# A decoder layer: routed tokens made on ScalarE and turned by the DMA, experts chosen on VectorE, layer norms applied on ScalarE

## The chip, the cores and the metric

One core of one Trainium2 chip. The metric is the device time of one execution in microseconds, the median of several runs. Another execution was profiled; its rows are quoted below.

## What is computed

A decoder layer on 2048 tokens (32 x 64) of width 256, in float32. Three parts, each on a layer norm of x and each added to x:

```python
x = x + attn(layernorm(x))          # 16 heads of 16; rope; each token's heads attend to each other (bshd,bstd->bsht)
x = x + xattn(layernorm(x), ctx)    # 16 heads, 2048 keys; q, k, v and the probabilities quantised to 8 bits
x = x + moe(layernorm(x))           # 8 experts of hidden 128, the best 2 of a token, and a shared one

scores = sigmoid(xt @ gate.T); sel = top_k(scores + expert_bias, 2)
xb = bfloat16(xt * score)           # the token times the score of each chosen expert
h = silu(xb @ w1[e].T) * (xb @ w3[e].T); out_r = h @ w2[e].T
hs = silu(xt @ shared_w1.T) * (xt @ shared_w3.T); out = hs @ shared_w2.T + sum of out_r
```

## The kernel before

**Tiles and lags.** The tokens are 16 tiles of 128. The keys and values are made first (some 100 us); then `over_tiles` runs `body(t)` for t = 0 to 17 on every engine. In `body(t)` the cross attention of tile t runs through its 16 heads h, and around it lies the work of other tiles: a = t + 2 (norm 0, own attention), n = t + 1 (own attention's end, norm 1, the queries), m = t - 1 (end of the cross attention, norm 2, the gates), o = t - 2 (the experts, the output). Each engine has its list, written by hand: for every h, in which order the calls for t, a, n, m and o stand. An engine goes through its list in order; semaphores tie the lists together. Norms are numbered 0, 1, 2 (`kind`).

**A head.** TensorE makes scores(h, 0) and scores(h, 1), each 128 tokens by 1024 keys, in one of two PSUM slots. VectorE evicts both to `score` with the running minimum (L1178) and makes the exponent's bias (L1188). ScalarE's `exp_head` (L865) makes 16-bit probabilities; `score` and `prob` are rings of 4. SP's `turn` (L431) issues a DMA transpose of 128x2048 two-byte elements for each head into one of 6 buffers. `times_values` (L1558) multiplies four heads at a time by the values.

**Norms.** VectorE gathers the statistics. GpSimd's `ln_scale` makes variance + eps (L462), its power -1/2 (L466) and, for all three norms (`POOL_NORMS`), the normed tokens `normed` (L482). TensorE turns them (`ln_turn`), ScalarE copies them to `normed_t` (`ln_keep`). After `ln_turn(1, n)` at h = 12 come `xq` (L1386 and L1502), VectorE's `largest_query` and `quantise_queries` at h = 13, TensorE's `q_turn`, and ScalarE's `keep_queries`.

**Own attention on GpSimd.** `rope`, then eight products of 128x1024 elements (L594), each folded twice (L604, L612); `reduce_scores` and `largest_score` on VectorE (h = 11, 14, 15) and `shift_scores` on GpSimd stand before ScalarE's `head_exp`, after which come the four value products. `spread_sums(m)`, among them, needs VectorE's `cross_sum(m)` (L1195, h = 3).

**Experts.** `gate_and_shared` at h = 10 gives the gate's logits and the shared hidden layer; ScalarE takes a tanh of each. GpSimd's `choose` ranks the eight scores with twelve small instructions on 128x64 elements at most. TensorE's `spread_gates` (L1605, h = 13 and 14) multiplies each expert's column, spread to 128 columns, with the identity, so that the gate of every token lies along a row of all partitions; ScalarE copies it (`keep_gates`, h = 12 and 13), and GpSimd's `route` multiplies the turned tokens `normed_t` by it into `routed_t` (two products of 128x1024). The last tile does this on VectorE (`choose_last`, L1210 to L1222, and `route_last`). `experts(i, j)` (L1386, 8 bf16 matmuls each) makes the first (j = 0) and the second (j = 1) hidden product of four experts: (0,0) at h = 14, (0,1) and (1,0) at h = 0 of the next tile, (1,1) at h = 1. ScalarE's `hidden_tanh(0)` stands at h = 14, `hidden_tanh(1)` at h = 0 ahead of that head's exp; VectorE's `expert_hidden(0)` at h = 0 and `(1)` at h = 1; `experts_out` and `add_out` at h = 2.

Of the kernel before, what the change touches and what calls it, by code (L numbers as in the profile page):

```python
# [45 lines left out]
P = 128  # L46
# [17 lines left out]
POOL_NORMS = (0, 1, 2)  # L64
# [37 lines left out]
def by_dma(n):  # L102
    return n % H in BY_DMA
# [32 lines left out]
def layer_kernel(nc, a):  # L136
    with ExitStack() as ctx:
# [14 lines left out]
        earlier = sb("earlier", [P, E, E])  # L152
# [87 lines left out]
        gate = sb("gate", [P, 3, E])  # L240
        ahead = sb("ahead", [P, E, E])
        beats = sb("beats", [P, E, E])
        ties = sb("ties", [P, E, E])
        routed_gate = sb("routed_gate", [P, E])
        last_gate = sb("last_gate", [P, 4, E])

        routed_both = sb("routed_both", [P, 2, E * D], BF16)
        gate_wide = routed_both[:, 0, :].bitcast(F32).rearrange("p (e q) -> p e q", e=E)
# [110 lines left out]
        last_chain = sem("last_chain")  # L359
        gate_spread = sem("gate_spread")  # L360
        gate_kept = sem("gate_kept")
        routed_kept = sem("routed_kept")
# [19 lines left out]
        def _(sp):  # L382
# [15 lines left out]
            for buf, name in ((w_o, "w_o"), (w_xq, "w_xq"), (b_xq, "b_xq"), (w_p, "w_p"),  # L398
                              (b_p, "b_p"), (w_gate, "w_gate"), (b_expert, "b_expert"),
                              (earlier, "earlier"), (w_s1, "w_s1"), (w_s3, "w_s3"),  # L400
                              (w_s2, "w_s2")):
                sp.dma_start(buf[:], a[name]).then_inc(w_loaded, 16)
# [29 lines left out]

            def body(t):
                for h in range(H):
                    if t.exists() and by_dma(h):
                        turn(h, t)
                    if h == 9 and (t + 3).exists():
                        load_x(t + 3)
                    if h == 4 and (t + -2).exists():
                        store(t + -2)  # L440
# [8 lines left out]
        def _(pool):  # L449
# [5 lines left out]
            def ln_scale(kind, t):  # L455
# [3 lines left out]
                if kind not in POOL_NORMS and (due := t.due(1)) is not None:  # L459
# [22 lines left out]
                pool.tensor_scalar(normed[:, kind, :], x, mean_var[:, kind, 0:1], rstd[:, kind:kind + 1],  # L482
                                   ALU.subtract, ALU.mult).then_inc(ln_done[kind], 1)
# [27 lines left out]

            def choose(t):


                pool.wait_ge(gate_tanhed, t.count(1, 1))
                pool.sem_inc(settled, 1)
                if (due := t.due(2)) is not None:
                    pool.wait_ge(gate_spread, due)
                    pool.sem_inc(settled, 1)
                sig, biased, rank = gate[:, 0, :], gate[:, 1, :], gate[:, 2, :]  # L520
                mine = biased.unsqueeze(2).to_broadcast([P, E, E])
                others = biased.unsqueeze(1).to_broadcast([P, E, E])
                pool.tensor_scalar(sig, gate_tanh[:], 0.5, 0.5, ALU.mult, ALU.add).then_inc(gate_chain, 1)
                pool.wait_ge(gate_chain, t.count(12, 1))
                pool.sem_inc(settled, 1)
                pool.tensor_tensor(biased, sig, b_expert[:], ALU.add).then_inc(gate_chain, 1)
                pool.wait_ge(gate_chain, t.count(12, 2))
                pool.sem_inc(settled, 1)
                pool.tensor_tensor(ahead[:], others, mine, ALU.subtract).then_inc(gate_chain, 1)
                pool.wait_ge(gate_chain, t.count(12, 3))  # L530
                pool.sem_inc(settled, 1)
                pool.tensor_scalar(ties[:], ahead[:], 0.0, None, ALU.is_equal).then_inc(gate_chain, 1)
                pool.tensor_scalar(beats[:], ahead[:], 0.0, None, ALU.is_gt).then_inc(gate_chain, 1)
                pool.wait_ge(gate_chain, t.count(12, 5))
                pool.sem_inc(settled, 1)
                pool.tensor_tensor(ties[:], ties[:], earlier[:], ALU.mult).then_inc(gate_chain, 1)
                pool.wait_ge(gate_chain, t.count(12, 6))
                pool.sem_inc(settled, 1)
                pool.tensor_tensor(beats[:], beats[:], ties[:], ALU.add).then_inc(gate_chain, 1)
                pool.wait_ge(gate_chain, t.count(12, 7))  # L540
                pool.sem_inc(settled, 1)
                pool.tensor_tensor(ties[:, :, 0:4], beats[:, :, 0:4], beats[:, :, 4:8], ALU.add
# [1263 lines left out]
```

## Time and profile before

| what | value |
|---|---|
| median of 3 runs | 1085.49 us (1084.84 to 1087.52) |
| the profiled execution | 1091.66 us, span 1089.9 us |
| VectorE (DVE) busy | 906.8 us, 83% |
| GpSimd (POOL) busy | 854.3 us, 78% |
| TensorE (PE) busy | 754.3 us, 69% |
| ScalarE (ACT) busy | 686.6 us, 63% |
| DMA transposes | 256 |

A busy time is the sum of an engine's instructions; a wait is shown with the instruction before which the engine stood idle, and with what released it.

### The profile page before, as it was taken

How to read it: one execution, taken by the hardware profiler on the slowest of the kernel's cores; microseconds unless marked ns; L12 is line 12 of the kernel's file. 1: busy time of each engine (PE TensorE's matmuls, PEld its weight loads, DVE VectorE, ACT ScalarE, POOL GpSimd, SP SyncE). 2: the span in 40 equal slices, each digit the busy share in tenths (PEclk: the TensorE clock that was granted, in tenths of full speed). 3: DMA queues.
4: the chain of work that ended last, by engine and by line, in shares of the span. 5: the costliest groups of instructions: out<-in, count | busy, mean ns of one | idle time of the engine just before them, and what ended most of it. 6: DMA issues, size and time to landing. Idle time of an engine off the chain costs nothing.

```text
span 1089.9 us, 21862 instructions
## 1 busy us (share of the span) xinstructions
PE 754.3 (69%) x7250; PEld 438.0 (40%) x7328; DVE 906.8 (83%) x1802; ACT 686.6 (63%) x843; POOL 854.3 (78%) x874
## 2 busy tenths in 40 slices
PE   7956667676667577676656777676768677677565
PEld 4533314344334344344333444344334344334244
DVE  4996889797979889796979889696978889798983
ACT  2534667675757667575768667575666667567761
POOL 7658989797988979797989979797988979763030
PEclk9975779897979989797989879797988979788988
DMA  6012879686986969596877869596876969588991
GB/s 221 1 39 66 163 130 171 125 166 116 167 146 121 168 117 167 111 168 118 163 143 138 159 117 172 106 168 117 162 146 118 178 115 168 97 160 150 165 175 24
DMA packets 540888, 147.71 MB, mean 136 GB/s; under 512 B 534116, under 2 KB 538727, under 8 KB 540391
## 3 DMA queue, kind: packets, MB, share of 16 engines
q1 hardware_dynamic: 540774, 146.31, 72.4%
q8 instruction: 58, 0.95, 0.4%
q14 instruction: 56, 0.45, 0.1%
HBM read 9.96 MB, written 2.10 MB: 11 GB/s over the span
## 4 chain that ended last, share of the span: by engine, by line
issue 31%; POOL 29%; PE 19%; DVE 16%; ACT 2%; POOLq 1%; DMA 1%; SPq 0%; DVEq 0%; ACTq 0%
POOL product L594 14%; DVE score L1178 8%; PE ps L1605 4%; PE ps L1386 4%; POOL normed L482 3%; PE ps_score L1528 3%; POOL folded L612 3%; POOL rstd L466 2%; POOL qk_sin L581 2%; PE ps_score L1386 2%; POOL qk_rot L583 2%; PE ps L1502 1%; PE ps L1507 1%; DVE q_parts L1161 1%; PE ps L1391 1%
## 5 line engine op out<-in xcount | busy, mean ns | idle before, releaser
L1178 DVE TENSOR_SCALAR_CACHE_REDUCE score<-ps_score,q_neg 128x1024 f32<-128x1024 f32 x512 | 636.4, 1276 | 92.6 <-PE ps_score L1528 92.6
L865 ACT ACTIVATE prob<-score,exp_bias 128x2048 uint16<-128x2048 f32 x256 | 512.1, 2001 | 100.8 <-DVE exp_bias L1188 94.5
L1528 PE MATMUL ps_score<-keys,queries 128*128 128x512 bf16 x946 | 319.9, 424 | 178.7 <-DVE score L1178 165.2
L1528 PEld LDWEIGHTS ps_score<-keys,queries 128*128 128x128 bf16 x1024 | 77.7, 103 | 308.9 <-DVE score L1178 239.3
L604 POOL TENSOR_TENSOR folded<-product 128x512 f32<-128x512 f32 x128 | 158.7, 1263 | 2.7 <-DVE hs L1114 1.7
L594 POOL TENSOR_TENSOR product<-hs_exp,v_tok 128x1024 f32<-128x1024 f32 x64 | 149.7, 2353 | 1.6 <-ACT hs_exp L830 1.6
L594 POOL TENSOR_TENSOR product<-qk_rot 128x1024 f32<-128x1024 f32 x64 | 149.0, 2342 | 0.2 <-POOL qk_rot L587 0.2
L567 POOL TENSOR_TENSOR routed_both<-normed_t,routed_both 128x1024 bf16<-128x1024 f32 x30 | 70.6, 2356 | 33.7 <-ACT routed_both L916 33.2
L612 POOL TENSOR_TENSOR folded<-folded 128x256 f32<-128x256 f32 x128 | 92.6, 746 | 0.0
L1391 PE MATMUL ps<-ident,normed 128*128 128x128 f32 x96 | 24.8, 347 | 89.1 <-POOL normed L482 82.5
L809 ACT COPY normed_t<-ps 128x256 f32<-128x256 f32 x48 | 17.6, 366 | 100.8 <-PE ps L1391 100.8
L1558 PEld LDWEIGHTS ps_pv<-prob_t,values 128*32 128x32 f16 x4096 | 60.1, 99 | 31.6 <-issue 31.6
L1558 PE MATMUL ps_pv<-prob_t,values 128*32 128x128 f16 x4096 | 71.4, 224 | 1.9 <-DMA prob_t<-prob 1.9
L1188 DVE TENSOR_SCALAR exp_bias<-low 128x1 f32<-128x1 f32 x256 | 53.9, 210 | 5.3 <-issue 0.3
L1391 PEld LDWEIGHTS ps<-ident,normed 128*128 128x128 f32 x96 | 12.0, 164 | 109.6 <-POOL normed L482 100.8
L916 ACT COPY routed_both<-ps 128x512 f32<-128x512 f32 x30 | 17.4, 584 | 60.0 <-PE ps L1605 59.7
L1386 PE MATMUL ps<-routed_both,w 128*128 128x128 bf16 x512 | 41.4, 227 | 18.2 <-POOL routed_both L567 13.9
L1605 PE MATMUL ps<-ident,routed_gate 128*128 128x128 f32 x256 | 54.0, 398 | 0.0
L1605 PEld LDWEIGHTS ps<-ident,routed_gate 128*128 128x128 f32 x256 | 52.1, 310 | 0.1
L1386 PEld LDWEIGHTS ps<-routed_both,w 128*128 128x128 bf16 x512 | 33.2, 102 | 41.5 <-POOL routed_both L567 28.8
L865 ACT ACTIVATION_READ_ACCUMULATOR prob<-score,exp_bias 128x1 f32 x256 | 48.2, 188 | 0.0
L462 POOL TENSOR_SCALAR var_eps<-mean_var 128x1 f32<-128x1 f32 x48 | 12.8, 267 | 38.8 <-DVE mean_var L1106 37.8
(138 smaller groups left out, 1216.2 us busy)
## 6 DMA issues: line engine op xcount, KB each, us to landing
prob_t<-prob SPq DMA_TRANSPOSE x256, 4.5
prob_t<-in_w SPq DMA_DIRECT2D x3, 1024.0 KB, 4.8
x_in<-in_x SPq DMA_DIRECT2D x16, 128.0 KB, 3.0
score<-in_cond_t SPq DMA_DIRECT2D x4, 512.0 KB, 6.9
out<-x_out SPq DMA_DIRECT2D x16, 128.0 KB, 2.5
w_qkv<-in_w_qkv SPq DMA_DIRECT2D x1, 768.0 KB, 4.2
early<-in_w_kv SPq DMA_DIRECT2D x1, 512.0 KB
w_s<-in_w_s SPq DMA_DIRECT2D x3, 128.0 KB
```

What stands on the lines that cost most here:

```text
L567: pool.tensor_tensor(routed_t[:, EG * i:EG * i + EG], normed_t[:, 2].unsqueeze(1).to_broadcast([P, EG, C, P]), gate_wide[:, EG * i:EG * i ...
L594: pool.tensor_tensor(product[:, i % 2], a_, b_, ALU.mult).then_inc(multiplied, 1)
L604: pool.tensor_tensor(folded[:, r], product[:, r, :, :, 0:HD // 2], product[:, r, :, :, HD // 2:HD], ALU.add).then_inc(fold_done, 1)
L612: pool.tensor_tensor(folded[:, r, :, :, 0:HD // 4], folded[:, r, :, :, 0:HD // 4], folded[:, r, :, :, HD // 4:HD // 2], ALU.add).then_inc( ...
L865: act.activation(prob[:, s, :].bitcast(U16), score[:, s, :], ACT.Exp, bias=exp_bias[:, s:s + 1], scale=-1.0, accum_out=prob_sum[:, t.par, ...
L1178: dve.tensor_scalar(score[:, s, HALF * i:HALF * i + HALF], ps_score[:, score_slot(t.count(H, h), i)].rearrange("p b k -> p (b k)"), q_neg[ ...
L1188: dve.tensor_scalar(exp_bias[:, s:s + 1], low[:, s, 0:1], low[:, s, 1:2], LN255, ALU.min, ALU.add).then_inc(bias_ready, 1)
L1386: mm = pe.matmul(out, lhs[c], rhs[c], start=start and c == 0, stop=stop and c == C - 1)
L1391: mm = pe.transpose(out[:, P * c:P * c + P], src[:, P * c:P * c + P], ident[:])
L1528: mm = pe.matmul(ps_score[:, score_slot(n, i), b, :], queries[:, t.par, h // 2, h % 2, :], keys[:, h // 2, k0:k0 + KEYS], start=True, stop ...
L1558: mm = pe.matmul(out[j], beside_zeros(values, i, h + j), prob_t[:, t.count(H, h + j) % KEPT, i, :], start=(i == 0 and first), stop=(i == T ...
L1605: mm = pe.matmul(bank[6 + i][:, P * e:P * e + P], routed_gate[:, EG * i + e:EG * i + e + 1] .to_broadcast([P, P]), ident[:], start=True, s ...
```

## The change

Four parts:

- `choose` runs on VectorE for every tile, at h = 10 ahead of the bias, with the six steps that `choose_last` had (the largest two by `max` and `match_replace`). GpSimd's `choose` and its table `earlier` go.
- `route(e, m)` is eight instructions on ScalarE, four at h = 12 and four at h = 13, each ahead of that head's exp: expert e's copy of the tokens `normed` (not turned), scaled by row. SP's `turn_routed(m)`, at h = 13 ahead of `turn(13)`, turns all eight by one DMA transpose of 128x2048 bf16. `spread_gates`, `keep_gates`, GpSimd's `route` and `route_last` go.
- GpSimd's `ln_scale` ends with a 128x1 `shift`; ScalarE's `ln_apply` makes `normed`: norm 0 at h = 1, norm 2 at h = 8, norm 1 at h = 10.
- The experts' calls stand later: `experts(0,0)` and `(0,1)` at h = 0 ahead of scores(0,0), `(1,0)` at h = 0, `(1,1)` at h = 2; `hidden_tanh(0)` and `(1)` at h = 1 and 2, ahead of those heads' exp; `expert_hidden(0)` and `(1)` at h = 1 (ahead of the evictions) and h = 2 (behind them); `experts_out` and `add_out` at h = 3; the store at h = 5. `queries_or_keys(0)` moves from h = 3 to h = 4, and `sum_turn` waits for `ln_keep(0)` of tile t + 3.

The core of the diff:

```diff
@@
+            def turn_routed(t):
+
+                sp.wait_ge(routed_made, t.count(E, E))
+                sp.sem_inc(settled, 1)
+                if (due := t.due(4)) is not None:
+                    sp.wait_ge(hidden_made, due)
+                    sp.sem_inc(settled, 1)
+                sp.dma_start_transpose(routed_t.rearrange("p e c q -> p (e c) q"),
+                                       routed_tok.rearrange("p e d -> p (e d)")).then_inc(routed_turned, 16)
+
             def body(t):
                 for h in range(H):
+                    if (t + -1).exists() and h == 13:
+                        turn_routed(t + -1)
...
-                if kind not in POOL_NORMS:
-                    pool.tensor_scalar(shift[:, kind:kind + 1], mean_var[:, kind, 0:1],
-                                       rstd[:, kind:kind + 1], -1.0, ALU.mult, ALU.mult
-                        ).then_inc(ln_shifted[kind], 1)
-                    return
-                if kind > 0:
-                    pool.wait_ge((one_done, two_done)[kind - 1], t.count(1, 1))
-                    pool.sem_inc(settled, 1)
-                if (due := t.due(1)) is not None:
-                    pool.wait_ge(ln_turned[kind], due)
-                    pool.sem_inc(settled, 1)
-                x = (x_in[:, t.par, :], x_one[:, t.par, :], x_two[:])[kind]
-                pool.tensor_scalar(normed[:, kind, :], x, mean_var[:, kind, 0:1], rstd[:, kind:kind + 1],
-                                   ALU.subtract, ALU.mult).then_inc(ln_done[kind], 1)
+                pool.tensor_scalar(shift[:, kind:kind + 1], mean_var[:, kind, 0:1],
+                                   rstd[:, kind:kind + 1], -1.0, ALU.mult, ALU.mult
+                    ).then_inc(ln_shifted[kind], 1)
...
+            def route(e, t):
+
+                if e == 0:
+                    act.wait_ge(gate_chain, t.count(6, 6))
+                    if (due := t.due(16)) is not None:
+                        act.wait_ge(routed_turned, due)
+                act.activation(routed_tok[:, e, :], normed[:, 2, :], ACT.Copy, scale=routed_gate[:, e:e + 1]
+                               ).then_inc(routed_made, 1)
...
-                    if o.exists() and h == 0:
-                        hidden_tanh(1, o)
+                    if o.exists() and h in (1, 2):
+                        hidden_tanh(h - 1, o)
...
+                    if m.exists() and h in (12, 13):
+                        for e in range(EG * (h - 12), EG * (h - 12) + EG):
+                            route(e, m)
...
+                    if m.exists() and h == 8:
+                        ln_apply(2, m)
+                    if n.exists() and h == 10 + late:
+                        ln_apply(1, n)
...
+                    if a.exists() and h == 1 + behind:
+                        ln_apply(0, a)
...
-                    if o.exists() and h == 0:
+                    if o.exists() and h == 1:
                         expert_hidden(0, o)
...
+            def experts(i, j, t):
+
+                b = ((5, 6), (7, 5))[i][j]
+                pe.wait_ge(routed_turned, t.count(16, 16))
+                if i == 1 and j == 0:
+
                     pe.wait_ge(shared_chain, t.count(2, 2))
-                for e in range(EG):
-                    mm = pe.matmul(bank[6 + i][:, P * e:P * e + P], routed_gate[:, EG * i + e:EG * i + e + 1]
-                                   .to_broadcast([P, P]), ident[:], start=True, stop=True)
-                mm.then_inc(gate_spread, 1)
-
-            def experts(i, j, t):
-
-                b = ((5, 6), (7, 5))[i][j]
-                pe.wait_ge(routed_kept, t.count(2, i + 1))
+                if i == 0 and j == 1:
+
+                    pe.wait_ge(two_done, t.count(1, 1))
...
                     if o.exists() and h == 0:
+                        experts(0, 0, o)
                         experts(0, 1, o)
                     if t.exists():
                         scores(h, 0, t)
...
-                    if m.exists() and h == 14:
-                        experts(0, 0, m)
```

VectorE's new `choose(t)` is the old `choose_last(t)` of the listing above with `gate` for `last_gate`, a count of 6 a tile on `gate_chain`, and for its last step a wait for the routes of the tile before.

## Rows read from the trace of the kernel before

**Rows 1.** Windows of one tile; busy time (instructions) by engine, granted clock, DMA share
```profile
core 0: us, PE busy (x) PEld busy (x) DVE busy (x) ACT busy (x) POOL busy (x), PEclk, DMA share, GB/s
249.78:311.25 61.47, 41.96 (x455) 24.75 (x449) 52.48 (x107) 41.20 (x51) 53.37 (x56) 0.89 0.81 142
...
864.06:925.48 61.42, 45.30 (x505) 26.90 (x511) 52.85 (x110) 41.51 (x52) 53.41 (x56) 0.88 0.79 146
```

**Rows 2.** The chain of waits, tile 6: start us, us, what
```profile
503.52 0.85 PE ps_score L1528 x2
504.38 1.71 PE ps L1386 x4
...
509.71 1.03 PE ps L1507 x8
510.75 3.31 PE ps L1605 x16
```

**Rows 3.** The timeline of VectorE, tiles 6 and 7, with idle time before
```profile
495.64 0.69 DVE L1114 TENSOR_REDUCE hs<-folded 128x128 f32<-128x512 f32 x1 [0.71 <-POOL folded L612]
...
504.42 1.28 DVE L1178 TENSOR_SCALAR_CACHE_REDUCE score<-ps_score,q_neg 128x1024 f32<-128x1024 f32 x1 [3.83 <-PE ps_score L1528]
...
507.27 0.43 DVE L1142 TENSOR_REDUCE ps<-ps 128x16 f32<-128x256 f32 x1 [1.31 <-PE ps L1502]
...
514.53 1.28 DVE L1178 TENSOR_SCALAR_CACHE_REDUCE score<-ps_score,q_neg 128x1024 f32<-128x1024 f32 x1 [2.22 <-PE ps_score L1528]
...
522.03 1.28 DVE L1178 TENSOR_SCALAR_CACHE_REDUCE score<-ps_score,q_neg 128x1024 f32<-128x1024 f32 x1
...
531.85 0.24 DVE L1195 RECIPROCAL sum_inv<-prob_sum 128x16 f32<-128x16 f32 x1
...
550.98 1.28 DVE L1178 TENSOR_SCALAR_CACHE_REDUCE score<-ps_score,q_neg 128x1024 f32<-128x1024 f32 x1
...
553.64 1.27 DVE L1178 TENSOR_SCALAR_CACHE_REDUCE score<-ps_score,q_neg 128x1024 f32<-128x1024 f32 x1
```

**Rows 4.** The timeline of GpSimd, tiles 6 and 7
```profile
502.86 0.20 POOL L523 TENSOR_SCALAR gate<-gate_tanh 128x8 f32<-128x8 f32 x1
...
507.88 2.47 POOL L604 TENSOR_TENSOR folded<-product 128x512 f32<-128x512 f32 x2
...
518.84 2.36 POOL L567 TENSOR_TENSOR routed_both<-normed_t,routed_both 128x1024 bf16<-128x1024 f32 x1
...
529.68 0.22 POOL L462 TENSOR_SCALAR var_eps<-mean_var 128x1 f32<-128x1 f32 x1
...
530.97 1.24 POOL L482 TENSOR_SCALAR normed<-x_in,mean_var,rstd 128x256 f32<-128x256 f32 x1 [0.31 <-POOL rstd L466]
...
534.48 0.52 POOL L509 COPY sum_wide<-sum_inv 128x128 f32<-128x128 f32 x2
```

**Rows 5.** The timeline at the end, the choice of the last tile and its experts
```profile
1076.88 0.17 DVE L1210 TENSOR_SCALAR last_gate<-gate_tanh 128x8 f32<-128x8 f32 x1 [5.30 <-ACT gate_tanh L904]
...
1077.89 0.17 DVE L1222 SCALAR_TENSOR_TENSOR routed_gate<-last_gate 128x8 f32<-128x8 f32 x1
...
1081.57 1.75 PE L1386 MATMUL ps<-routed_both,w 128*128 128x128 bf16 x24 [0.33 <-DVE routed_both L1229]
```

**Rows 6.** The timeline of ScalarE, tile 6
```profile
513.08 2.04 ACT L847 COPY queries<-ps 64x1024 bf16<-64x1024 bf16 x2
...
518.91 0.42 ACT L830 ACTIVATE hs_exp<-hs 128x256 f32<-128x256 f32 x1 [0.71 <-POOL hs L488]
519.24 1.99 ACT L865 ACTIVATE prob<-score,exp_bias 128x2048 uint16<-128x2048 f32 x1
```

**Rows 7.** The DMA queues (packets, MB, share) and `prob_t`'s transposes
```profile
q1 hardware_dynamic: 540774, 146.31, 72.4%
...
DMA to landing us min/median/max: 4.2/4.5/7.5
```

**Rows 8.** The timeline near the end: expert matmuls, the tanh behind them
```profile
1056.34 1.06 PE L1386 MATMUL ps<-routed_both,w 128*128 128x128 bf16 x16
...
1060.12 0.58 ACT L923 ACTIVATE early<-ps 128x512 f32<-128x512 f32 x1
```

More of the change, by code:

```diff
@@ L63 @@
 TURN = 2
-POOL_NORMS = (0, 1, 2)
 BY_DMA = tuple(range(H))
@@ L458, in ln_scale @@
                 pool.sem_inc(settled, 1)
-                if kind not in POOL_NORMS and (due := t.due(1)) is not None:
+                if (due := t.due(1)) is not None:
                     pool.wait_ge(ln_done[kind], due)
@@ L668, in body @@
                     ln_scale(1, n)
-                if m.exists() and t.exists():
-                    choose(m)
                 if a.exists():
@@ L975, in _ @@
             first, second = Tile(0), Tile(1)
-            if 0 not in POOL_NORMS:
-                ln_apply(0, first)
+            ln_apply(0, first)
             ln_keep(0, first)
@@ L984, in _ @@
                     head_exp(first)
-                if u == 5 and 0 not in POOL_NORMS:
+                if u == 5:
                     ln_apply(0, second)
@@ L994, in _ @@
                 if u == 9:
-                    if 1 not in POOL_NORMS:
-                        ln_apply(1, first)
+                    ln_apply(1, first)
                     ln_keep(1, first)
@@ L1204, in cross_norm, with choose @@
                                   xo_raw[:].rearrange("p c q -> p (c q)"), ALU.mult).then_inc(xo_done, 1)
-            def choose_last(t):
-                sig, biased, marked, best = (last_gate[:, i, :] for i in range(4))
+            def choose(t):
+                sig, biased, marked, best = (gate[:, i, :] for i in range(4))
                 dve.wait_ge(gate_tanhed, t.count(1, 1))
-                dve.tensor_scalar(sig, gate_tanh[:], 0.5, 0.5, ALU.mult, ALU.add).then_inc(last_chain, 1)
-                dve.wait_ge(last_chain, 1)
+                dve.tensor_scalar(sig, gate_tanh[:], 0.5, 0.5, ALU.mult, ALU.add).then_inc(gate_chain, 1)
+                dve.wait_ge(gate_chain, t.count(6, 1))
@@ L1325, in body @@
                         ln_combine(1, n)
-                    if o.exists() and h == 1:
+                    if o.exists() and h == 2:
                         expert_hidden(1, o)
-                    if m.exists() and not t.exists() and h == 14:
-                        route_last(1, m)
-                    if m.exists() and not t.exists():
-                        if h == 10:
-                            choose_last(m)
-                        if h == 13:
-                            route_last(0, m)
-                    if o.exists() and h == 2:
+                    if m.exists() and h == 10:
+                        choose(m)
+                    if o.exists() and h == 3:
                         add_out(o)
@@ L1646, in body @@
                         pe.wait_ge(values_half, 2)
-                    if m.exists() and h == 14:
-                        spread_gates(1, m)
                     if o.exists() and h == 0:
+                        experts(0, 0, o)
                         experts(0, 1, o)
@@ L1688, in body @@
                         times_values(3 * G, m)
-                    if m.exists() and h == 13:
-                        spread_gates(0, m)
                     if a.exists() and h == 4 + behind:
+                        queries_or_keys(0, a)
                         queries_or_keys(1, a)
-                    if a.exists() and h == 3 + behind:
-                        queries_or_keys(0, a)
                     if t.exists() and h == 7:
```

143 lines of the change are left out of this document (25 added, 118 removed).

## The prediction

> **What bounds the kernel now.** I start with the windows, one for each tile of the main loop [rows 1]. Eleven neighbouring ones last about 61.45 us each; VectorE is busy for 52.5 of them, GpSimd for 53.4, TensorE for 42, ScalarE for 41, and the DMA engines for 0.8 of the time. The two busiest each have some 8 us idle in every tile, so the pace is set by a ring of waits and not by one full engine. The chain of waits of one tile [rows 2] gives the ring: GpSimd's layer norm 1 (its end is 502.8, where `choose` begins [rows 4]), TensorE's turn of it, the scores and `xq`, VectorE's `quantise_queries`, `q_turn`, `spread_gates`, then VectorE up to `largest_score` and back to GpSimd. VectorE's timeline has what it waited in this tile [rows 3]: 0.71, 3.83, 1.31 and 2.22 us, all on that ring. 61.45 - 8.07 = 53.4 us is what VectorE needs for a tile without waits. A plain head (two evictions and a bias) is 553.64 - 550.98 = 2.66 of it.
>
> **What leaves, per tile.** GpSimd [rows 4]: the twelve instructions of `choose`, 502.86 to 507.88, 5.0 us; two `route` products of 2.36; and each of three norms ends with a 128x1 instruction in place of a 128x256 one: 1.24 + 0.31 of hand-over against 0.22 (as `var_eps`) + 0.2, so 1.1 less. Its own work falls from 53.4 to about 40. TensorE: the 16 f32 matmuls of `spread_gates`, 3.31 on the ring [rows 2].
>
> **What comes.** VectorE: `choose`, which the last tile already runs as `choose_last`, 1076.88 to 1078.06 = 1.18 us [rows 5]. ScalarE: three `ln_apply` and eight `route`, 128x256 f32 each, priced by `hs_exp` of that shape: 0.42 long, the next instruction starts 0.33 after it [rows 6]. That is 3.6 us a tile, less two gate copies; from 41 it doesn't fill ScalarE. DMA: a 17th transpose of 128x2048 two-byte elements. One takes 4.2 to 7.5 us to land, median 4.5 by the issues' list, and occupies 0.724 x 1089.9 / 256 = 3.1 us of the 16 DMA engines [rows 7]; 17 are 52 us a tile, not full either. On SP the new one stands ahead of `turn(13)`, whose probabilities are made after the routed tokens, so nothing waits behind it.
>
> The Trainium skill (DMA: Bandwidth & Descriptors, section Latency and other measured facts) gives DMA transposes 261 GB/s in a non-contiguous case, an estimate of 2.0 us for these 0.52 MB. The trace doesn't agree (3.1 us). By the page the wait B below would be 1.1 shorter and the result 13 us lower.
>
> **The new ring.** Engines are in order, so I follow the calls' new places through one steady tile, in four pieces.
>
> A, from `shift` of norm 1 on GpSimd to VectorE being ready for head 0 of the next tile. ScalarE has `ln_apply(1)` at h = 10 ahead of `gate_tanhs`, and VectorE has `choose` at h = 10 ahead of bias(10): so VectorE now waits there for GpSimd's norm 1. Apply 0.35, tanh 0.25, choose 1.18, bias 0.13: at 1.9. Head 11 with `reduce_scores` 0.6 and `shared_hidden` 0.53: 5.7. Head 12: 8.3. TensorE stood idle until 3.8 and then runs at the slow clock, as after the long wait of before [rows 2]: scores 0.85, turn 0.7 (502.8 to 503.5), scores 0.85 and `keep` 0.4, `xq` 2.9 (504.38 to 507.27): the product is there at about 9.1, so VectorE waits 0.8. Quantise 2.4 (507.27 to 509.71), heads 13, 14, 15 at 2.66, one reduce 0.6, `largest_score` 0.34: 20.3.
>
> B, the new wait at h = 0. `experts(0,0)` and `(0,1)` stand ahead of scores(0,0) on TensorE and need the whole transpose. `q_turn` is done at 12.5, ScalarE's `keep_queries` takes 2.04 [rows 6], four routes 1.4: 16.0. SP issues, 4.5 to land: 20.6. Sixteen expert matmuls 1.06 [rows 8], the first scores 0.6: 22.4. VectorE wanted them at 20.3: 2.1 late; 1.8 with the fastest landing of the trace, 5.1 with the slowest.
>
> C, from there to `cross_sum` at h = 3. Before: 522.03 to 531.85 = 9.8 [rows 3]. `expert_hidden(0)` has moved behind head 0: +1.3. It needs `hidden_tanh(0)`, which stands on ScalarE behind exp_head(0), and that one waits for bias(0) of VectorE: so VectorE stands for an exp 2.0 [rows 6], a tanh 0.6 [rows 8] and the hand-overs, 2.7 us. `expert_hidden(1)` needs a tanh behind exp_head(1) and `keep_xo` (2.1 + 0.3 + 0.6 + 0.1), against 2.4 of evictions: 0.7 more. C is 14.5.
>
> D, GpSimd from there to `shift` of norm 1. Before: 534.48 [rows 4] to 502.8 + 61.45 = 564.25, 29.8 with two norms and no wait inside; less 2 x 1.1: 27.6. `choose` and the routes stood behind norm 1, so D doesn't get shorter by them. The stretch from `largest_score` to `spread_sums` does, but there GpSimd now waits for `cross_sum`, which hangs on C: what it saves turns into idle time.
>
> Sum: 20.3 + 2.1 + 14.5 + 27.6 = 64.5, against 61.45: +3.05 a tile. From the other side: VectorE's 53.4 + 1.2, and waits of 2.1 (B), 2.7 and 0.7 (C), 0.8 (xq), and 3.7 at `choose`, where VectorE is at 14.5 + 7 x 2.66 + 3.5 of other work + 2.4 = 39.0 after head 0 and the tanh at 42.1 + 0.6: 64.6. Twelve tiles (2 to 13) have all of it: +37.
>
> The ends. Tiles 0 and 1: fewer norms on GpSimd, -2, and the first B, +2. Tile 14: 2.7 + 0.7 + 1.3 + 2.1, less a wait behind `spread_gates` as the 2.22 of [rows 3]: +4.6. Tile 15: 4.7, less some 1.3 of waits for `route`: +3.4. After the last head, `hidden_tanh(1)`, `expert_hidden(1)` and `experts_out` of tile 14 lie in front of `cross_norm` (0.6 + 1.4 + 0.6 and hand-overs, +3); the last norm is 0.7 shorter; and from `choose` to the experts there are eight routes and a transpose, 2.7 + 4.6, where there were 1081.57 - 1078.06 = 3.5 [rows 5]: +3.8. Together +6.
>
> 37 + 0 + 4.6 + 3.4 + 6 = +51. The profiled execution took 1091.66 (span 1089.9 and 1.8 around it), its like would take 1143; it lies 6 above the median of the runs, 1085.49, and on that the forecast is 1136.
>
> **Rivals.**
> 1. The transpose is hidden: B is 0, the ring 62.4, +11 for twelve tiles and +13 at the ends, 1110. For it: the DMA queue is free at that point. Against: the routes stand behind `keep_queries`, which ends at 14.6 of A's 20.3, and a landing takes 4.2 at least.
> 2. VectorE becomes the bound and the new waits on it are small: faster. It waited 8.07; with 1.2 for `choose`, the kernel is faster as soon as the new waits sum to under 6.9 a tile. With 2 us of them a tile is 56.6, 58 us less over twelve, 1040 with the ends. For it: GpSimd loses 13 of its 53.4 us. Against: the 2.7 at h = 1 follows from the order of calls alone, and with B and 0.7 there are 5.5 before GpSimd comes in.
> The Trainium skill (Perfetto Trace Analysis, section Identifying the Most-Contended Engine) takes the engine with the highest occupancy for the one to relieve; here it is GpSimd by 1 us, and the page by itself would point to this rival.
> 3. GpSimd has slack that I don't see: VectorE's own chain with C and B, 62.2, +9 and +15 at the ends, 1110.
> 4. Transposes crowd each other and land near 7.5, and TensorE, idle more often, is granted the slow clock in more places: the ring is 67.5, 1172.
>
> **Numbers.** Forecast 0.60, rivals 1 and 3 together 0.17, rival 2 0.11, rival 4 0.12. Rivals 1 and 3 are slower by 2%; errors in both at once give no change, which I take 0.05 for. A measurement of this kernel tells 0.3% (3.3 us) from none. So faster 0.12, within 0.3% 0.05, slower 0.83. The range for 8 in 10 leaves out rival 2 and the far end of 4: 1100 to 1165.
>
> **What would show it.** In the changed trace: tiles of 64 to 65 us; GpSimd busy about 40 of each, with its longest wait before `sum_wide`; VectorE idle 2.7 us at h = 1 before `early`, released by ScalarE's tanh; VectorE idle before head 0, released by scores that stood behind the experts; VectorE idle some 3.7 before `gate`, released by `gate_tanh`; and no wait of 3.8 us before head 12. I am wrong if a tile is under 61.4 us, above all if the tanh at h = 1 is there when VectorE asks for it, or the transpose has landed when TensorE gets to the experts.

## The result, and the profile after

| what | before | after |
|---|---|---|
| median | 1086.03 us (1084.84 to 1087.52, 4 runs) | 1180.36 us (1178.57 to 1187.96, 4 runs) |
| ratio | | 1.0881, interval 1.083 to 1.0933 |
| profiled execution | 1091.66 us, span 1089.9 | 1178.77 us, span 1177.0 |
| VectorE, GpSimd busy | 906.8, 854.3 us | 917.2, 693.0 us |
| granted TensorE clock, mean | 0.865 | 0.806 |

Slower, as forecast, but by 94 us and not by 51; the time is above the range. Some runs of a kernel fall into a slower state of the chip: the medians below count them and the ratios don't, which bears on `norms_alone` alone, where two of six did. The changed kernel's windows of one tile, with the columns of [rows 1]:

```profile
core 0: us, PE busy (x) PEld busy (x) DVE busy (x) ACT busy (x) POOL busy (x), PEclk, DMA share, GB/s
474.54:540.63 66.09, 43.59 (x372) 23.58 (x360) 51.72 (x110) 43.31 (x60) 42.54 (x41) 0.84 0.78 139
540.63:608.12 67.49, 44.92 (x433) 23.82 (x436) 53.63 (x117) 44.73 (x60) 42.81 (x41) 0.80 0.78 137
```

A tile takes 66.1 and 67.5 us where it took 61.45. GpSimd did lose load: 42.5 of a tile instead of 53.4. (The forecast had 40: it took 5.0 off for `choose`, which is its time with the gaps between the instructions; `choose_alone` below shows 3.0 of work.) VectorE, now the busiest engine of a tile, stands idle for 14 us of each instead of 9. Its timeline shows where, with the idle time and its releaser in the brackets. The lines with a wait over 0.25 us are shown, and two more; those between are left out. It answers to [rows 3]:

```profile
525.64 0.17 DVE L1137 TENSOR_SCALAR gate<-gate_tanh 128x8 f32<-128x8 f32 x1 [4.03 <-ACT gate_tanh L828]
533.41 0.43 DVE L1069 TENSOR_REDUCE ps<-ps 128x16 f32<-128x256 f32 x1 [0.17 <-PE ps L1417]
547.59 1.28 DVE L1105 TENSOR_SCALAR_CACHE_REDUCE score<-ps_score,q_neg 128x1024 f32<-128x1024 f32 x1 [2.69 <-PE ps_score L1443]
553.32 0.69 DVE L1155 SCALAR_TENSOR_TENSOR early<-early,ps 128x512 f32<-128x512 f32 x1 [2.78 <-ACT early L849]
561.62 0.69 DVE L1155 SCALAR_TENSOR_TENSOR early<-early,ps 128x512 f32<-128x512 f32 x1 [1.76 <-ACT early L849]
563.08 0.24 DVE L1122 RECIPROCAL sum_inv<-prob_sum 128x16 f32<-128x16 f32 x1
592.31 0.17 DVE L1137 TENSOR_SCALAR gate<-gate_tanh 128x8 f32<-128x8 f32 x1 [4.36 <-ACT gate_tanh L828]
```

These are the waits that the prediction named: at `choose` 4.03 (forecast 3.7), before head 0 2.69 (2.1), the first tanh 2.78 (2.7), the second 1.76 (0.7; the mean of ten tiles is 1.96). The waits of 3.83, 2.22 and 0.71 of [rows 3] are gone, and the one before `quantise_queries` is 0.17 instead of 1.31. The wait before head 0 can be followed back through TensorE's and ScalarE's timelines and the list of issues:

```profile
538.77 1.71 ACT L842 ACTIVATE routed_both<-normed,routed_gate 128x256 bf16<-128x256 f32 x4
...
545.53 1.16 PE L1301 MATMUL ps<-routed_both,w 128*128 128x128 bf16 x16 [2.22 <-DMA routed_both<-routed_both]
```

```profile
540.63 4.85 DMA routed_both<-routed_both
545.53 1.16 PE ps L1301 x16
546.70 0.87 PE ps_score L1443 x2
...
552.69 0.60 ACT early L849
553.32 0.70 DVE early L1155
```

```profile
DMA to landing us min/median/max: 4.3/4.7/5.6
```

The second fence is the chain of waits, and the third the transposes of the routed tokens, against 4.2/4.5/7.5 of [rows 7]. The last routes end at 540.48; the transpose is on its way from 540.63 and takes 4.85, with TensorE waiting for it; the experts run, and only then the scores that VectorE wants.

On GpSimd the time saved is a wait, as the prediction's D has it. Three lines of its timeline, answering to [rows 4]:

```profile
524.64 0.26 POOL L474 TENSOR_SCALAR shift<-mean_var,rstd 128x1 f32<-128x1 f32 x1 [0.20 <-POOL rstd L470]
542.09 0.62 POOL L481 TENSOR_TENSOR hs<-hs,hs_max 128x256 f32<-128x256 f32 x1 [10.51 <-DVE hs_max L1046]
563.58 0.52 POOL L502 COPY sum_wide<-sum_inv 128x128 f32<-128x128 f32 x2 [4.72 <-DVE sum_inv L1122]
```

It waits for `largest_score` (10.5) and for `cross_sum` (4.7): about 15 us that the lighter GpSimd gives back in one tile.

The four pieces of the ring, as means of ten tiles (3 to 12), cut at instructions of VectorE's and GpSimd's timelines. Piece A is counted here from the start of norm 1's `rstd`, some 1 us before the end of its `shift`, so in these terms the forecast A is 21.3 and D 26.6.

| piece, us | before | forecast | after |
|---|---|---|---|
| A, norm 1 to VectorE ready for head 0 | 20.06 | 21.3 | 20.98 |
| B, to the start of head 0's eviction | 1.41 | 2.1 | 2.82 |
| C, to `cross_sum` | 9.89 | 14.5 | 15.68 |
| D, GpSimd to the next norm 1 | 30.06 | 26.6 | 27.18 |
| a tile | 61.42 | 64.5 | 66.66 |

(Before, B held `expert_hidden(0)`, which belongs to C after.) The spans differ by 87.1: tiles 2 to 13 +64.0 (forecast 37), tile 14 +7.0 (4.6), tile 15 +9.6 (3.4), what follows it +9.8 (6), tiles 0 and 1 +1.0 (0), the part before the loop -4.3. The prediction had nothing for that last one.

### The profile page after: what moved, and what is told of

Its sections match the earlier page's. It is cut to its first block, busy times and chain, and to the rows that moved or that the text cites. A ratio compares the mean times of both kernels' runs of the same rounds, so it can differ in the third digit from the quotient of the medians.

```text
span 1177.0 us, 21273 instructions
## 1 busy us (share of the span) xinstructions
PE 782.0 (66%) x7072; PEld 424.2 (36%) x7072; DVE 917.2 (78%) x1905; ACT 750.1 (64%) x989; POOL 693.0 (59%) x664
## 4 chain that ended last, share of the span: by engine, by line
issue 24%; DVE 23%; PE 19%; POOL 18%; ACT 8%; DMA 7%; SPq 1%; POOLq 0%; DVEq 0%; ACTq 0%
DVE score L1105 13%; POOL product L527 10%; DMA routed_both<-routed_both 6%; PE ps L1301 6%; PE ps_score L1443 4%; PE ps_pv L1473 2%; ACT routed_both L842 2%; POOL qk_sin L514 2%; POOL folded L545 2%; DVE early L1155 2%; PE ps_score L1301 2%; ACT queries L771 2%; ACT early L849 2%; POOL qk_rot L516 1%; POOL rstd L470 1%
## 5 line engine op out<-in xcount | busy, mean ns | idle before, releaser
L1443 PE MATMUL ps_score<-keys,queries 128*128 128x512 bf16 x1024 | 378.8, 466 | 256.9 <-DVE score L1105 249.6
L481 POOL TENSOR_TENSOR hs<-hs,hs_max 128x256 f32<-128x256 f32 x16 | 9.9, 621 | 149.4 <-DVE hs_max L1046 149.4
L1473 PE MATMUL ps_pv<-prob_t,values 128*32 128x128 f16 x4096 | 92.2, 261 | 3.2 <-DMA prob_t<-prob 3.2
L1473 PEld LDWEIGHTS ps_pv<-prob_t,values 128*32 128x32 f16 x4096 | 78.8, 118 | 34.5 <-issue 34.5
L502 POOL COPY sum_wide<-sum_inv 128x128 f32<-128x128 f32 x32 | 8.4, 291 | 139.7 <-DVE sum_inv L1122 139.7
L1155 DVE SCALAR_TENSOR_TENSOR early<-early,ps 128x512 f32<-128x512 f32 x32 | 22.0, 687 | 84.2 <-ACT early L849 74.0
L1301 PE MATMUL ps<-routed_both,w 128*128 128x128 bf16 x512 | 53.6, 278 | 46.9 <-DMA routed_both<-routed_both 45.3
L1301 PEld LDWEIGHTS ps<-routed_both,w 128*128 128x128 bf16 x512 | 46.6, 129 | 72.5 <-DMA routed_both<-routed_both 56.2
L842 ACT ACTIVATE routed_both<-normed,routed_gate 128x256 bf16<-128x256 f32 x128 | 54.2, 494 | 0.3
L1137 DVE TENSOR_SCALAR gate<-gate_tanh 128x8 f32<-128x8 f32 x16 | 2.7, 172 | 58.4 <-ACT gate_tanh L828 58.4
```

The source lines that it names most:

```text
L842: act.activation(routed_tok[:, e, :], normed[:, 2, :], ACT.Copy, scale=routed_gate[:, e:e + 1]).then_inc(routed_made, 1)
L1155: dve.scalar_tensor_tensor(out=th, in0=th, scalar=1.0, in1=first_, op0=ALU.add, op1=ALU.mult).then_inc(chain, 1)
L1301: mm = pe.matmul(out, lhs[c], rhs[c], start=start and c == 0, stop=stop and c == C - 1)
L1443: mm = pe.matmul(ps_score[:, score_slot(n, i), b, :], queries[:, t.par, h // 2, h % 2, :], keys[:, h // 2, k0:k0 + KEYS], start=True, stop ...
L1473: mm = pe.matmul(out[j], beside_zeros(values, i, h + j), prob_t[:, t.count(H, h + j) % KEPT, i, :], start=(i == 0 and first), stop=(i == T ...
```

## The experiments

**Theory 1:** the order of calls makes the ring. Three calls stand ahead of something that VectorE needs sooner: `ln_apply(1)`, which waits for GpSimd, ahead of the gate's tanh; the experts, which wait for the DMA, ahead of the scores; `expert_hidden(0)`, which waits for ScalarE, ahead of the evictions. **Theory 2:** the parts cost time by themselves: VectorE's extra work, the extra transpose, ScalarE's extra instructions. **Theory 3:** TensorE's lower granted clock is what went beyond the forecast. All ratios are to the kernel before on the same chip (its own median moves by a few us between chips), with 95% intervals; the changed kernel's is 1.0881.

**One move each, and all three.** They undo nothing of the four parts and only change the place of a call.

```diff
+ gate_first: ScalarE, h = 10, behind gate_tanhs and shared_tanhs instead of ahead
+                    if n.exists() and h == 10 + late:
+                        ln_apply(1, n)
+ scores_first: TensorE, h = 0, behind scores(0, 0) and scores(0, 1) instead of ahead
+                        experts(0, 0, o)
+                        experts(0, 1, o)
                         experts(1, 0, o)
+ evict_first: VectorE, h = 1, behind the evictions instead of ahead
+                    if o.exists() and h == 1:
+                        expert_hidden(0, o)
```

> The changed kernel, with one call moved on ScalarE: norm 1's apply stands behind the two gate tanhs at h = 10 and no longer ahead of them. Theory 1 (the order of calls on the ring): VectorE stands before `choose` for 4.0 to 4.4 us in every tile for GpSimd's norm 1 only because of that place. Without it `choose`, head 11 and half of head 12 run while GpSimd works; the queries then come about 2.9 us sooner in the ring, 12 to 13 times: 1180 falls by some 36, to 1144 (range 1130 to 1155). Theory 2 (the engines themselves: ScalarE's and the DMA's added work, or the slow TensorE clock, cost the time, wherever the calls stand): the wait moves to the queries and nothing is gained, 1175 to 1185.

> The changed kernel, with the experts' first two products on TensorE at h = 0 behind that head's scores and no longer ahead of them. Theory 1: the wait for the DMA of the routed tokens (2.2 us idle, 2.8 with the matmuls) no longer holds VectorE's head 0; the experts are still done before ScalarE gets to their tanh. 2.8 a tile, in 14 tiles: minus 39, to 1141 (1130 to 1155). Theory 2: the transpose lands late because of DMA traffic and everything behind the experts waits just as long: 1175 to 1185, with the idle time of VectorE now before `early`.

> The changed kernel, with VectorE's first expert product at h = 1 behind that head's two evictions and no longer ahead of them. Theory 1: the 2.78 us idle before it (bias(0), exp, tanh) is covered by 2.4 us of evictions; `cross_sum` and with it GpSimd come 2.4 us sooner in 14 tiles: minus 33, to 1147 (1135 to 1160). Theory 2: the wait moves to the second expert product or to TensorE, 1175 to 1185.

> All three moves at once: gate tanhs ahead of norm 1's apply, scores ahead of the experts, evictions ahead of the first expert product. Theory 1: the gains add as long as the ring stays the bound, 2.9 + 2.8 + 2.4 = 8.1 a tile, until VectorE's own work (53.4 + 1.2) and its small waits bound it at some 58: 1075 to 1090, level with the kernel before or a little faster. Theory 2 (the engines): above 1150.

| kernel | median us | ratio | A | B | C | D |
|---|---|---|---|---|---|---|
| `gate_first` | 1153.19 | 1.0616 [1.0568, 1.0663] | 18.41 | 3.08 | 15.80 | 27.19 |
| `scores_first` | 1145.68 | 1.0544 [1.0514, 1.0574] | 21.31 | 0.10 | 15.57 | 27.19 |
| `evict_first` | 1135.38 | 1.0463 [1.0387, 1.0539] | 21.03 | 2.54 | 12.61 | 27.19 |
| `all_three` | 1077.07 | 0.9927 [0.99, 0.9954] | 18.59 | 0.10 | 13.52 | 27.22 |

Each move shortens the piece that it was aimed at, by 2.6, 2.7 and 3.1 us, and leaves the others within 0.4. The gains are 27, 35 and 45 us, 107 in sum; together they give 103, and the kernel with the whole change is then 0.7% faster than the one before. VectorE's waits, in total, times and longest, of `gate_first`, `scores_first`, `evict_first` and `all_three`, after those of the changed kernel:

```profile
DVE early L1155 <- ACT early L849: 74.0, 30, 7.3
DVE gate L1137 <- ACT gate_tanh L828: 58.4, 15, 4.8
DVE score L1105 <- PE ps_score L1443: 58.1, 47, 4.1
```

```profile
DVE early L1155 <- ACT early L849: 75.4, 29, 7.0
DVE score L1105 <- PE ps_score L1443: 60.6, 41, 4.9
...
DVE gate L1137 <- ACT gate_tanh L828: 4.8, 1, 4.8
```

```profile
DVE early L1155 <- ACT early L849: 71.9, 29, 6.9
DVE gate L1137 <- ACT gate_tanh L828: 58.5, 15, 4.8
DVE score L1105 <- PE ps_score L1443: 21.8, 37, 3.1
```

```profile
DVE score L1105 <- PE ps_score L1443: 59.2, 46, 4.2
DVE gate L1137 <- ACT gate_tanh L828: 58.5, 15, 4.8
DVE early L1155 <- ACT early L849: 28.2, 17, 7.0
```

```profile
DVE early L1155 <- ACT early L849: 37.5, 16, 7.0
DVE score L1105 <- PE ps_score L1443: 22.1, 37, 3.2
...
DVE gate L1137 <- ACT gate_tanh L828: 4.8, 1, 4.8
```

The first fence is the changed kernel's. In each of the next three one of the three totals has dropped and the other two stand within 2.5 us of where they were; in the last one all three are down. They are separate waits on one ring, which is why their gains add up.

**The rest of C.** The second tanh waits behind `keep_xo`, which waits for TensorE. `four_moves` is `all_three` with it ahead; `five_moves` also puts norm 0 one head later.

```diff
+ four_moves: ScalarE, h = 1, right behind exp_head(1), ahead of keep_xo
+                    if o.exists() and h == 1:
+                        hidden_tanh(1, o)
+ five_moves: ScalarE, ln_apply(0) at h = 2 and ln_keep(0) at h = 3 instead of 1 and 2
```

> The three moves of all_three, and a fourth: on ScalarE the second experts' tanh stands right behind exp_head(1) and ahead of `keep_xo`, which waits for TensorE's `times_values`. In all_three VectorE still stands 2.1 us before the second expert product in every tile, and GpSimd now has over 10 us of idle time in each, so VectorE's own list is the bound. Theory 1 (order of calls): most of the 2.1 goes, 1.5 to 2.0 in 14 tiles, 1077 becomes 1050 to 1058. Theory 2 (another bound, ScalarE or the DMA, has taken over): within 3 us of 1077.

> The four moves, and a fifth: on ScalarE norm 0's apply and keep stand one head later (h = 2 and 3), so exp_head(1) no longer waits for GpSimd's norm 0. In four_moves VectorE still stood 1.8 us before the second expert product, because exp_head(1), ahead of that tanh, started 2 us late behind the apply. If that is the reason why the fourth move gave 4 us where 20 were expected, most of the 1.8 goes now: 1073 becomes 1048 to 1058. If something else (the keep behind TensorE's turn at h = 3) takes its place, 1068 to 1076.

`four_moves` took 1073.38 us (0.9868 [0.9827, 0.9908]), and missed. Its ScalarE timeline and VectorE's show why:

```profile
513.54 0.60 ACT L725 ACTIVATE normed<-x_in,shift,rstd 128x256 f32<-128x256 f32 x1 [2.71 <-POOL shift L474]
514.05 1.99 ACT L789 ACTIVATE prob<-score,exp_bias 128x2048 uint16<-128x2048 f32 x1
516.04 0.57 ACT L849 ACTIVATE early<-ps 128x512 f32<-128x512 f32 x1
```

```profile
516.64 0.69 DVE L1157 SCALAR_TENSOR_TENSOR early<-early,ps 128x512 f32<-128x512 f32 x1 [1.84 <-ACT early L849]
```

`keep_xo` is out of the way, but now the head's exp starts late: it stands behind `ln_apply(0)`, which stood idle for 2.71 us until GpSimd had its `shift`. The changed kernel has the same wait (3.31 at 556.60), but there it isn't a link of the ring: exp_head(1) starts 0.29 behind the apply's end and is released by VectorE's bias, in each of tiles 3 to 13. It became one when the evictions were put ahead of the first expert product and the bias came sooner. `five_moves`, which takes it away, took 1062.71 (0.9751 [0.9726, 0.9776]): C falls from 13.52 in `all_three` to 11.60 and a tile to 58.05. It is 5 us above its expectation; D has risen by 0.6 to 27.86.

`six_moves` puts `ln_apply(1)` of that kernel at h = 11, right ahead of the copy that uses it.

> five_moves with the same move of norm 1's apply to h = 11, right ahead of its keep. GpSimd's norm 1 comes later than exp_head(10) could start, so exp_head(10) and the keep both come sooner, as in norms_placed, but here VectorE has nearly no wait left (0.8 us for the queries): minus 4 to 12, 1051 to 1059.

It took 1063.3 (0.978 [0.9758, 0.9802]): no gain, where 4 to 12 us were expected, although ScalarE no longer waits before that apply (3.4 in most tiles of `five_moves`, nothing in `six_moves`). What takes that time instead wasn't followed.

**The parts alone.** `choose_alone` is the kernel before with `choose` on VectorE at h = 10 for every tile; `spread_gates` and `route` stay.

```diff
-                if m.exists() and t.exists():
-                    choose(m)
...
+                    if m.exists() and h == 10:
+                        choose_last(m)
```

> The kernel before, with one part of the change alone: `choose` of every tile on VectorE at h = 10; routes, spread, copies and norms stay as they were. It takes 5.0 us a tile from GpSimd and gives VectorE 1.2. Theory 1 (the ring): GpSimd's `choose` stood behind norm 1, not on the ring, and VectorE's new 1.2 falls into the 3.8 us that it waits for norm 1's queries: 1083 to 1090. Rival (GpSimd's load is the bound, as its 53.4 busy us of 61.45 suggest): 4 to 5 us a tile, 1020 to 1040.

1092.79 us (1.0046 [1.0023, 1.0069]). GpSimd's twelve instructions, 5.0 us a tile with the gaps between them, are gone, its busy time falls from 854.3 to 807.0 (3.0 a tile), and nothing is gained; the median is 3 us above what was expected. Its waits and its timeline show that the time went into a wait which had 33.2 us in the whole kernel before, 1.83 in the tile of [rows 4]:

```profile
POOL routed_both L567 <- ACT routed_both L914: 125.1, 15, 19.2
```

```profile
505.48 2.34 POOL L567 TENSOR_TENSOR routed_both<-normed_t,routed_both 128x1024 bf16<-128x1024 f32 x1 [7.88 <-ACT routed_both L914]
```

GpSimd's 53.4 us per tile were thus not the bound of the kernel before. VectorE's busy time rose by 2.4 a tile (906.8 to 945.4) and not by 1.2: `choose`'s last step took 1.19 on average, against 0.17 in `choose_last`, and why isn't shown. So the run doesn't say what the relief of GpSimd alone would be worth.

By the Trainium skill (Perfetto Trace Analysis, section Identifying the Most-Contended Engine) the engine with the highest occupancy is to be optimised first. In a tile of the kernel before that was GpSimd, by 1 us. Taking 3 us a tile of `choose` from it gained nothing; taking 2.8 of the norms from it, in `norms_alone` below, gained 2.5%. The occupancy was the same guide for both; what told them apart was whether the work lay on the ring.

`spare_transpose` is the kernel before with one more transpose of 128x1792 two-byte elements per tile, at the place of `turn_routed`, into a buffer that nothing reads.

```diff
+                sp.dma_start_transpose(spare[:], keys[:, 0, 0:P * (T - 2)]).then_inc(spare_turned, 16)
```

> The kernel before, with a DMA transpose of 128x1792 bf16 elements added in each tile at h = 13 ahead of turn(13), from the keys into a spare buffer that nothing reads: what the 17th transpose costs by itself, when nothing waits for it. Theory 1: it only delays turn(13) by up to 3 us, which has slack: 1085 to 1092. Rival (the transposes crowd each other and this is what made the changed kernel slow): above 1110.

1089.27 us (1.0001 [0.9976, 1.0026]), with this row for its queue (packets, MB, share):

```profile
q1 hardware_dynamic: 569958, 153.65, 75.7%
```

The share rises from 72.4% and the time doesn't: the transpose as a load costs nothing that could be measured. Its price in the changed kernel is the wait for its landing.

`norms_alone` is the kernel before with only the norms' last step on ScalarE; `norms_back` is the changed kernel, and `five_norms_back` is `five_moves`, with that step back on GpSimd.

```diff
-POOL_NORMS = (0, 1, 2)
+POOL_NORMS = ()
...
+                    if m.exists() and h == 8:
+                        ln_apply(2, m)
+                    if n.exists() and h == 10 + late:
+                        ln_apply(1, n)
...
+                    if a.exists() and h == 1 + behind:
+                        ln_apply(0, a)
```

> The kernel before, with the norms alone on ScalarE, at the places of the changed kernel (norm 0 at h = 1, 2 at h = 8, 1 at h = 10 ahead of the gate tanhs); `choose` and `route` stay on GpSimd. Theory 1 (the ring): GpSimd's part of the ring is 3 x 1.1 shorter a tile, the apply costs 0.6, and norm 1's keep now waits for exp_head(10), +1.6: about 1 us a tile is left, 1070 to 1086. Rival (every us taken from GpSimd counts): 3 us a tile, below 1050. Rival (moving norms to ScalarE is itself what made the changed kernel slow): above 1100.

> The changed kernel, with its norms back on GpSimd (the form of the kernel before); choose on VectorE, the routes on ScalarE, the transpose and the late experts stay. ScalarE's gate tanhs no longer stand behind a wait for GpSimd, so VectorE's wait before `choose` goes, as in gate_first (-27); GpSimd's part is 2.2 a tile longer, the apply (0.6) and the wait of the keep for exp_head(10) go. Theory 1: 1148 to 1168. If the norms were the larger part of the loss: below 1130.

> The five moves with the norms back on GpSimd. In the moved order GpSimd has some 10 us of idle time in each tile before `hs`, so 3.3 us more of work on it should be hidden: within 6 us of five_moves. If GpSimd's load still sets the pace: 20 us or more slower.

| kernel | median us | ratio | A | B | C | D |
|---|---|---|---|---|---|---|
| `norms_alone` | 1066.38 | 0.9745 [0.9688, 0.9803] | 19.24 | 1.41 | 9.89 | 28.05 |
| `norms_back` | 1160.3 | 1.0653 [1.0624, 1.0682] | 18.80 | 2.38 | 15.80 | 28.27 |
| `five_norms_back` | 1078.21 | 0.9899 [0.9876, 0.9922] | 18.63 | 0.10 | 11.58 | 29.43 |

Moving the norms to ScalarE takes 2.0 us out of D and 0.8 out of A on the kernel before, and is worth 2.5% there. That is more than was expected (1070 to 1086): the expectation had A longer by the apply and by the wait for exp_head(10), and it is shorter. In `five_moves` it takes 1.6 out of D and is worth 15.5 us (expected within 6, a miss: D stayed on the ring although GpSimd had waits elsewhere). In the changed kernel the same step costs 20 us: D is 1.1 shorter with it, but one of its calls holds up `choose` and A is 20.98, and 18.80 without it. The sign of that part hangs on where one call of 0.6 us stands and on what stands behind it: in `norms_alone` the call has the same place ahead of the gate's tanh, but there VectorE has no `choose` that needs the tanh. `norms_placed` is `norms_alone` with that call one head later:

```diff
-                    if n.exists() and h == 10 + late:
+                    if n.exists() and h == 11 + late:
                         ln_apply(1, n)
```

> norms_alone with norm 1's apply at h = 11 (behind exp_head(10), right ahead of its keep) and not at h = 10. The ring gets norm 1's turned tokens 1.6 us sooner, since the keep no longer waits for an exp that starts behind the apply: 1066 becomes 1040 to 1052. If exp_head(10) was never in the way: within 4 us of 1066.

1053.29 us (0.968 [0.9654, 0.9706]), 1 us above what was expected and the fastest version here. Its lead on `norms_alone` is in the profile (A is 18.60, a tile 58.03 against 58.59) and smaller than expected (0.6 a tile, not 1.6); in the ratios the intervals of the two overlap. Its ScalarE timeline:

```profile
482.63 1.99 ACT L865 ACTIVATE prob<-score,exp_bias 128x2048 uint16<-128x2048 f32 x1
484.71 0.60 ACT L798 ACTIVATE normed<-x_one,shift,rstd 128x256 f32<-128x256 f32 x1
485.84 0.37 ACT L809 COPY normed_t<-ps 128x256 f32<-128x256 f32 x1 [0.53 <-PE ps L1397]
```

Here the apply starts with no idle time before it. In the other steady tiles it waits up to 1.4 us for `shift`, where in `norms_alone` it waits 2.9 to 4.0.

**The clock.** `filled` is the changed kernel with matmuls on TensorE whose results nothing reads: 8 at h = 0 ahead of the experts, where it waits for the transpose, 40 at h = 11 behind the scores. `filled_more` has 28 more at h = 1, and `experts(1, 0)` behind them.

```diff
+            def fill(k):
+                for _ in range(k):
+                    pe.matmul(bank[6][:, 256:512], ident_bf[:], keys[:, 0, 0:256], start=True, stop=True)
...
                     if o.exists() and h == 0:
+                        fill(8)
                         experts(0, 0, o)
...
+                    if m.exists() and h == 11:
+                        pe.wait_ge(two_done, m.count(1, 1))
+                        fill(40)
```

> The changed kernel, with products that nobody reads added on TensorE where it stands idle: 8 of 128x256 bf16 at h = 0 ahead of the experts, 40 at h = 11 behind that head's scores. They keep TensorE busy through two of its three long idle times. If the slow TensorE clock behind the waits (granted 0.806 on average, 0.865 before) is a part of the loss, norm 1's queries and head 0's scores come sooner by 1 to 2 us a tile although TensorE has more to do: 1150 to 1168. If the clock plays no part: 1180 to 1200, the fillers' own time.

> The filled kernel, with `experts(1,0)` at h = 1 behind that head's scores and 28 more unread products (128x256 bf16) ahead of it, in TensorE's third long idle time (5.3 us at h = 1). If the slow clock behind that idle time is why the second half of the piece up to `cross_sum` took 1.2 us more than forecast: the piece falls from 15.4 to 14.5 or 14.7 and the kernel from 1166 by 8 to 15, to 1151 to 1158. If it is the order of calls alone: within 4 us of 1166, or slower by the fillers.

| kernel | median us | ratio | granted clock | A | B | C | D |
|---|---|---|---|---|---|---|---|
| `filled` | 1165.84 | 1.072 [1.067, 1.077] | 0.864 | 20.84 | 2.06 | 15.44 | 27.20 |
| `filled_more` | 1154.32 | 1.0617 [1.0592, 1.0643] | 0.891 | 20.50 | 2.32 | 14.93 | 27.20 |

More work for TensorE, and the kernel is 14.5 and 26 us faster. With the mean clock at 0.864, as before the change, B is 2.06, which is the forecast. `filled_more` changes a place too, so its last 11.5 us aren't the clock's alone; neither run says how much of the 26 us the filling itself takes back.

What the clock does to C can be read within one kernel. The second tanh stands behind `keep_xo`, which waits for TensorE's `times_values` (L1473). In the changed kernel TensorE stands idle for 5.3 us ahead of scores(1, 0) and then runs at the lower of its two levels (1.2 GHz, shown as 0.50), as a rule through `times_values` too, which then takes 1.90 us; in the tile shown above it came back up within it:

```profile
556.60 0.60 ACT L725 ACTIVATE normed<-x_in,shift,rstd 128x256 f32<-128x256 f32 x1 [3.31 <-POOL shift L474]
557.49 2.00 ACT L789 ACTIVATE prob<-score,exp_bias 128x2048 uint16<-128x2048 f32 x1 [0.29 <-DVE exp_bias L1115]
...
560.72 0.37 ACT L809 COPY xo_raw<-ps_pv 128x256 f32<-128x256 f32 x1 [1.14 <-PE ps_pv L1473]
```

Windows around `times_values`, one of the changed kernel, then two of neighbouring tiles of `filled_more` (columns as in the first windows above; the granted clock is the third number from the end):

```profile
488.86:494.36 5.50, 4.87 (x77) 2.96 (x78) 4.23 (x9) 2.69 (x3) 3.06 (x3) 0.50 0.21 41
544.43:549.93 5.50, 4.43 (x78) 2.97 (x79) 4.24 (x9) 2.90 (x4) 3.06 (x3) 0.69 0.22 43
610.22:615.72 5.50, 4.07 (x84) 2.54 (x84) 4.92 (x10) 3.45 (x5) 3.08 (x3) 1.00 0.20 39
```

`times_values` took 1.90, 1.66 and 1.08 us in them, and C was 15.87, 15.65 and 14.24. `filled_more` has tiles of both kinds: six of tiles 3 to 13 have the full clock and a C of 14.2, the other five 15.6. In the six `keep_xo` doesn't wait, and VectorE waits 0.5 us for the second tanh.

## Why the prediction was wrong in size and right in kind

- **The mechanism held.** VectorE is idle at the four places that the prediction named, released by what it named; GpSimd's saving became waits; the singles and `all_three` show that the waits are separate and come from the order of calls. Tiles take 66.7, not 64 to 65.
- **The failed step is the sum of the ring's new waits,** and in it the terms C and B. C was forecast at 14.5 and measured 15.68: the second tanh's wait was 1.96 as a mean and not 0.7. The working had `keep_xo` at 0.3 with no wait for TensorE, and showed no reason for that; it waits 1.1 to 1.5 in most tiles for `times_values`, which TensorE makes at the lower clock behind its own idle time at h = 1. In six tiles of `filled_more`, with the full clock, C is 14.2 and the wait 0.5, and in the other five, at a lower clock, 15.6 and 1.9: the term is the clock's. `ln_apply(0)` holds exp_head(1) in `all_three` and `four_moves`, not here. B was forecast at 2.1 and measured 2.82; in `filled`, with TensorE's granted clock back at 0.864, it is 2.06. D is 0.6 longer and A 0.3 shorter than forecast. In sum +2.2 a tile, 27 of the 36 us by which the profiled execution exceeds the 1143 that was forecast for it.
- **The ends** make up the other 9: tile 14 +2.4, tile 15 +6.2, what follows +3.8, less 3.3 at the start. At the very end the forecast had 2.7 for eight routes and 4.6 for the transpose:

```profile
1159.31 3.29 ACT L842 ACTIVATE routed_both<-normed,routed_gate 128x256 bf16<-128x256 f32 x8
...
1167.09 1.14 PE L1301 MATMUL ps<-routed_both,w 128*128 128x128 bf16 x9 [7.99 <-DMA routed_both<-routed_both]
```

  The routes took 3.3, with the shared layer's tanh ahead of them. In tile 15 one wait was not in the forecast, 3.15 us for the scores, with TensorE just out of a long wait:

```profile
1106.81 1.28 DVE L1105 TENSOR_SCALAR_CACHE_REDUCE score<-ps_score,q_neg 128x1024 f32<-128x1024 f32 x1 [3.15 <-PE ps_score L1443]
```

  The rest of tile 15's 6.2 wasn't divided further.
- **Rival 1 and rival 3** didn't come about: TensorE waited 2.22 for the transpose in the tile shown, and D was on the ring. **Rival 2**, faster with small waits, is what the order of calls stood in the way of: `five_moves` has the whole change, tiles of 58.05 us and 1062.7. Of GpSimd's lost load, `choose` alone gained nothing and the norms alone 2.5%; the routes' part was never run alone.
- **Rival 4** was half right, and the ring, 66.7, came out nearer to its 67.5 than to the 64.5 forecast. Its clock was most of the ring's overshoot: 0.8 of a tile in B by `filled`, and C's 1.2 by the tiles of `filled_more`, of 2.2 in all. That went beyond what the forecast took the lower clock for, which was the stretch up to `xq`. Its crowded transposes weren't there: the routed tokens landed in 4.3 to 5.6 us.
- **The median.** The forecast took 6 us off, as the profiled execution of before lay 6 above the median of the runs; the one of after lies 1.6 below its median (1178.77 against 1180.36). That is the last 8 of the 44 us between 1136 and 1180. The ring's 27 alone would have stayed within the range, at 1163; with the ends and these 8 it left it.

## What to carry to other kernels

When work is moved between engines that go through lists in order, list for every new instruction what it waits for and what stands behind it: here the same four parts took 1180 us in one order and 1063 in another, and three moves of a call or two were worth 103 us. An engine with the most busy time need not be the bound; test it by taking some of its work away, and mind where that work lies: 3 us a tile of `choose` off GpSimd gained nothing, 2.8 of the norms 2.5%. Ask of each new idle time of TensorE at which clock the work behind it runs, and who waits for that work. Measure the parts of a change one at a time: one of the parts, well placed, gave 1053 us, less than all four in the best order tried (1063).

## What the runs showed of the hardware

- ScalarE on 128x256 f32: `hs_exp` took 0.42 us [rows 6]; the routes, with a scale per row, took 1.71 for four and 3.29 for eight, (3.29 - 1.71) / 4 = 0.40 for each more; `normed`, with scale and bias per row, took 0.60. The prediction had 0.33 from one to the next for all of them. Whether the operands or the function make the difference wasn't tried.
- Unread matmuls made a kernel faster. The mean granted clock went from 0.806 to 0.864 and 0.891, and the median from 1180.4 to 1165.8 and 1154.3 us. The same 64 matmuls of `times_values` took 1.90 us at a granted clock of 0.50 and 1.08 at 1.00.
- One DMA transpose more per tile moved the DMA share from 72.4% to 75.7% and the time not at all (1.0001 [0.9976, 1.0026]).
